# GpSimd's tap powers, VectorE's first statistics, the gated end and filler matmuls put in another order

## The reference

```python
def tblock(x, ...):                      # 4 heads of 8 channels, L0
    net = mha(x, qkv_w, proj_w, proj_b, rel_table, rel_idx) + x
    net = layernorm(net, ln_g, ln_b)
    return (net @ fc1_w.T + fc1_b) @ fc2_w.T + fc2_b + net

def L1(x, ...):
    h = einsum('bdl,de->ble', u, W_enc) + b_enc             # 32 -> 256
    dtA = A * dt[:, None]; Bd = (exp(dtA) - 1.0) / A
    vand = exp(dtA[:, :, None] * arange(16))
    K = 2.0 * einsum('dn,dnl->dl', Cc * Bd, vand).real      # 16 taps per channel
    y = gelu(causal_conv(h, K) + D * h)
    g = y @ W_glu + b_glu
    g = g[..., :256] * sigmoid(g[..., 256:])
    return layernorm(h + g, ln_gamma, ln_beta) @ W_dec + b_dec   # 256 -> 32

x = x + L0(group_norm(x))
x = x + L1(group_norm(x))
```

## Time and profile before

| | us |
|---|---|
| runs | 230.51, 227.83, 230.13 |
| median | 230.13 |
| the profiled execution | 230.15 |
| its span in the profile | 228.3 |
| PE, DVE, ACT, POOL busy | 196.2, 148.5, 128.2, 102.7 |
| filler matmuls (L1752), 84 of them, busy | 25.0 |
| mean granted TensorE clock | 0.924 |

### The profile page before, as it was taken

How to read it: one execution, slowest core, us unless ns; L and a number is a source line. 1 busy time by engine, 2 the same in 40 slices (tenths; PEclk the granted TensorE clock), 3 DMA queues, 4 the chain that set the end, 5 groups by cost and what they waited for, 6 DMA issues and landing times.

```text
span 228.3 us, 6295 instructions
## 1 busy us (share of the span) xinstructions
PE 196.2 (86%) x2533; PEld 103.2 (45%) x2533; DVE 148.5 (65%) x300; ACT 128.2 (56%) x248; POOL 102.7 (45%) x220
## 2 busy tenths in 40 slices
PE   0859989899896669898849877999999999999985
PEld 0334444445553224344335343445555566665582
DVE  0876566947654873649815698994233568898873
ACT  2273976775565663765503825873455765566550
POOL 6258443637860504707797230630000256776540
PEclk9985599999999985999958999999999999999985
DMA  5944500000000000200000000153000000000000
GB/s 169 190 122 106 122 3 4 4 3 3 3 0 3 0 3 3 90 6 3 4 0 4 0 0 3 34 132 78 0 0 0 0 3 1 14 10 10 10 13 20
DMA packets 3905, 6.70 MB, mean 29 GB/s; under 512 B 1605, under 2 KB 2869, under 8 KB 3781
## 3 DMA queue, kind: packets, MB, share of 16 engines
q1 hardware_dynamic: 2581, 3.91, 7.3%
q0 software_dynamic: 512, 1.37, 2.3%
q10 hardware_dynamic: 784, 1.03, 2.0%
HBM read 4.53 MB, written 0.40 MB: 22 GB/s over the span
## 4 chain that ended last, share of the span: by engine, by line
PE 59%; DVE 14%; issue 9%; POOL 8%; ACT 7%; DMA 2%; SPq 0%; DVEq 0%; POOLq 0%; ACTq 0%
PE ps L1864 13%; PE ps L1899 12%; PE ps L1752 3%; PE ps L1666 3%; DVE qs L1175 2%; PE ps L1644 2%; DVE ks L1175 2%; PE ps L1626 2%; PE ps L1687 2%; PE ps L1710 2%; PE ps L1656 2%; PE ps L1614 2%; DMA sel<-pick 2%; DVE x L1275 2%; PE ps L1935 2%
## 5 line engine op out<-in xcount | busy, mean ns | idle before, releaser
L1752 PE MATMUL ps<-fill 128*128 128x512 f16 x84 | 25.0, 416 | 5.9 <-DMA sel<-pick 5.9
L1216 DVE TENSOR_REDUCE mx<-ps 128x16 f32<-128x784 f32 (+3 forms) x18 | 15.9, 889 | 17.6 <-PE ps L1626 17.6
L882 ACT ACTIVATE pr<-ps 128x784 f32<-128x784 f32 (+3 forms) x18 | 13.7, 759 | 13.3 <-PE ps L1666 13.3
L764 POOL TENSOR_TENSOR pr<-pr 128x448 f16<-128x448 f32 x7 | 7.5, 1070 | 27.0 <-ACT pr L1061 27.0
L855 ACT CAST q_hi<-ps 128x392 f16<-128x392 f32 (+1 forms) x30 | 13.8, 511 | 10.1 <-PE ps L1580 9.6
L1037 ACT ACTIVATE pt<-ps,ybias 128x448 f32<-128x448 f32 x14 | 8.9, 634 | 13.0 <-PE ps L1864 12.0
L1899 PE MATMUL ps<-vm_buf,wglu_hi 128*128 128x448 f16 x56 | 15.1, 352 | 0.0
L1275 DVE STREAM_TRANSPOSE x<-u 96x448 f32<-96x448 f32 (+4 forms) x12 | 13.9, 1155 | 2.0 <-ACT u L935 1.7
L1752 PEld LDWEIGHTS ps<-fill 128*128 128x128 f16 x84 | 7.8, 107 | 14.3 <-issue 9.0
L1864 PE MATMUL ps<-u4hi,gw_hi 128*128 128x448 f16 x56 | 12.9, 353 | 1.6 <-ACT u4hi L1019 1.5
L895 ACT ACTIVATE den<-ps 128x196 f32<-128x196 f32 (+2 forms) x15 | 5.2, 346 | 15.6 <-PE ps L1692 15.6
(11 more groups left out here) (274 smaller groups left out, 544.0 us busy)
## 6 DMA issues: line engine op xcount, KB each, us to landing
xr<-x SPq DMA_DIRECT2D x3, 392.0 KB, 6.1
wglu<-w_glu POOLq DMA_DIRECT2D x1, 512.0 KB, 3.9
x<-x_win SPq DMA_DIRECT2D x4, 112.0 KB, 3.6
out<-u SPq DMA_DIRECT2D x7, 56.0 KB, 1.6
x<-x_win SPq DMA_DIRECT2D x2, 168.0 KB, 4.8
u4hi<-ust_s SPq DMA_DIRECT2D x4, 84.0 KB, 2.4
par_g<-stage_g POOLq DMA_DIRECT2D x1, 274.5 KB, 3.1
x<-x_win ACTq DMA_DIRECT2D x2, 112.0 KB, 6.3
```

Of the source, the lines that this page charges most:

```text
L882: nc.scalar.activation(dst[:, :, 0:cw], ps[:, 2:4, 0:cw], ACT.Exp).then_inc(s_exp[k], 1)
L1216: nc.vector.tensor_reduce(m[:, :, 0:n], ps[:, bank:bank + 2, 0:n * T].rearrange("p h (j m) -> p h j m", m=T), AX.X, ALU.max).then_inc(s_mx ...
L1752: nc.tensor.matmul(ps[:, 3, :], fill[:, 0:128], fill[:, :], start=True, stop=True)
```

## The change

It moves work and adds no arithmetic that the output needs. Its parts are:

1. GpSimd: level 1 of the tap powers runs ahead of `norm_halves("g", 0)`, and `wencst` is split behind `norm_halves("g", 1)`.
2. TensorE: the eight transposes of `gt` move from group 2 of block g to group 3, the last, ahead of its first `attend`.
3. TensorE: twelve more fillers at the front of each block: four between the bias matmuls and the products of the first scores, four ahead of the first turned scores, four ahead of the first bias matmuls of group 1.
4. VectorE, front: the tables from `sel` are split in two; the image's statistics come first, the sums of `sel` (`pick_sums`) behind them, `negsel` and `mask` (`pick_tables`) after `spread_projection("b")`. `repeat32` is made in `pick_sums`. TensorE's first fillers no longer wait for `sel`; there are 9 ahead of the statistics' matmul instead of 7, and 12 behind it, tied to two stages of the group norm, instead of 8.
5. The first half of block b's weights is issued as GpSimd's first instruction, not from ScalarE's queue.
6. Gated end, last chunk only: VectorE's `token_scale(n-2)` comes behind `gated_residual(n, 1)`, and TensorE's `decoded_back` of that chunk behind `mean_square_of_sum` of the last but one.

```diff
--- before.py
+++ after.py
...
+            pool.dma_start(par["b"][0:96, 0:288], stage_b[0:96, 0:288]).then_inc(s_pb, 16)
             nc.gpsimd.memset(eps[:, :], 1e-5).then_inc(s_eps, 1)
...
+            def enc_weights():
...
                 nc.gpsimd.tensor_copy(wencst[:, :], s4("wenc", 96)).then_inc(s_we, 1)
...
             first_tap()
...
-            tap_powers((0,))
+            tap_powers((0, 1))
             norm_halves("g", 0)
-            tap_powers((1, 2, 3))
+            tap_powers((2, 3))
             tap_weights()
             norm_halves("g", 1)
+            enc_weights()
             dec_weights()
...
-            act.dma_start(par["b"][0:96, 0:288], stage_b[0:96, 0:288]).then_inc(s_pb, 16)
...
             def group_norm_by_quarters():
...
-                nc.vector.tensor_tensor(repeat32[:, :], sel[:, 0:96], sel[:, 32:128], ALU.add)
...
+                pick_sums()
                 dve.wait_ge(s_gnm, 1)
...
-            def attention_constants():
+            def key_rows():
...
                 ins.then_inc(s_key, 1)
+                dve.wait_ge(s_key, 1)
+                for i in range(2):
+                    ins = nc.vector.tensor_copy(ones[:, i, :].rearrange("p (r w d) -> p r w d", r=2, w=2),
+                                                key_of[:, i, :].unsqueeze(1).unsqueeze(3).broadcast_to([128, 2, 2, 8]))
+                ins.then_inc(s_const, 1)
+            def pick_sums():
                 dve.wait_ge(s_sel, 16)
+                nc.vector.tensor_tensor(repeat32[:, :], sel[:, 0:96], sel[:, 32:128], ALU.add).then_inc(s_const, 1)
                 residue = sel[:, 0:64]
...
                 nc.vector.tensor_reduce(half_of[:, :], residue.rearrange("p (a l) -> p a l", a=2), AX.X,
...
-                dve.wait_ge(s_const, 1)
+            def pick_tables():
+                dve.wait_ge(s_const, 3)
                 nc.vector.tensor_scalar(negsel[:, :, :], head_of[:, :].unsqueeze(2).broadcast_to([128, HEADS, 64]),
...
                 nc.vector.scalar_tensor_tensor(out=mask[:, :].rearrange("p (j a) -> p j a", a=2),
...
-                                               op0=ALU.mult, op1=ALU.mult)
-                dve.wait_ge(s_key, 1)
-                for i in range(2):
-                    ins = nc.vector.tensor_copy(ones[:, i, :].rearrange("p (r w d) -> p r w d", r=2, w=2),
-                                              key_of[:, i, :].unsqueeze(1).unsqueeze(3).broadcast_to([128, 2, 2, 8]))
-                ins.then_inc(s_const, 1)
-                dve.wait_ge(s_const, 2)
+                                               op0=ALU.mult, op1=ALU.mult).then_inc(s_const, 1)
...
             def spread_max(k, g):
...
                 dve.wait_ge(s_mx[k], 2 * g + 2)
+                dve.wait_ge(s_const, 4)
...
-            attention_constants()
+            key_rows()
             group_norm_by_quarters()
...
                     spread_projection("b")
+                    pick_tables()
...
                 gated_residual(n, 0)
-                if n >= 2:
+                if 2 <= n < last:
                     token_scale(n - 2)
                 gated_residual(n, 1)
+                if n == last:
+                    token_scale(n - 2)
                 residual_lo(n)
                 if n >= 2:
...
                 nw = wide(k, g)
+                if u == 2:
+                    keep_running(4, bank)
...
                                      bt[k][:, h, 0:1, 0:T].broadcast_to([128, nw, T]), start=True, stop=True)
+                if u == 0:
+                    keep_running(4)
...
-                pe.wait_ge(s_const, 2)
+                pe.wait_ge(s_const, 4)
                 pe.wait_ge(s_mxe[k], g + 1)
...
-            def keep_running(count):
+            def keep_running(count, bank=3):
...
-                    nc.tensor.matmul(ps[:, 3, :], fill[:, 0:128], fill[:, :], start=True, stop=True)
+                    nc.tensor.matmul(ps[:, bank, :], fill[:, 0:128], fill[:, :], start=True, stop=True)
...
             def tap_weights():
...
             pe.wait_ge(s_fill, 1)
-            pe.wait_ge(s_sel, 16)
-            keep_running(7)
+            keep_running(9)
+            pe.wait_ge(s_const, 2)
             pe.wait_ge(s_gn, 3)
             nc.tensor.matmul(ps[0:96, 2, 0:2], repeat32[:, :], mean_q[:, :], start=True, stop=True).then_inc(s_gnm, 1)
-            keep_running(8)
+            keep_running(4)
+            pe.wait_ge(s_gnr, 3)
+            keep_running(5)
+            pe.wait_ge(s_uhi["b"], 1)
+            keep_running(3)
...
                 for g in range(groups[k]):
+                    if g == 0:
+                        keep_running(4)
                     turned_scores(k, g, 0)
...
                         scores(k, g + 1, 1)
-                    if k == "b" and g == last:
-                        fold_constant("g")
+                    if g == last:
+                        if k == "b":
+                            fold_constant("g")
+                        else:
+                            pe.wait_ge(s_mx[k], 2 * groups[k])
+                            tap_weights()
                     attend(k, g, 0)
...
-                    if g == last - 1:
+                    if k == "b" and g == last - 1:
                         pe.wait_ge(s_mx[k], 2 * groups[k])
-                        if k == "b":
-                            fold("g")
-                        else:
-                            tap_weights()
+                        fold("g")
...
-                if n >= 2:
+                if 2 <= n < last:
                     decoded_back(n - 2)
             decode(last - 1)
             mean_square_of_sum(last - 1)
+            decoded_back(last - 2)
             decode(last)
...
```

## The result

| | before | changed |
|---|---|---|
| runs, us | 230.51, 227.83, 230.13, 231.29 | 220.49, 219.06, 220.61, 219.88 |
| median | 230.32 | 220.19 |
| the profiled execution | 230.15 | 220.49 |
| its span | 228.3 | 218.7 |
| mean granted clock of it | 0.924 | 0.966 |

The changed kernel is faster: the ratio is 0.958, with a 95% interval of 0.953 to 0.963. The forecast was 220.2 us.

The account below looks back on a forecast made before the run. TensorE was taken to bound the kernel, busy 86% of the span, losing time in waits and 27.3 us at half clock. Gains of 5.5 + 2.2 + 2.0 + 0.3 = 10.0 us from 230.15 gave 220.2 us, range 217.0 to 225.5.

Parts of the forecast that it names:

- C: Front of block b: products start 0.65 us earlier and the slow stretch goes or shrinks; −2.0 us, bounds −6.5 and +1.2.
- B: Front of block g: twelve fillers keep the clock at 2.4 GHz; −2.2 us, bounds −3.4 and +2.7.
- A: Taps, block g: level 1 fills GpSimd's pause, so gt, yn and the feed-forward come earlier; −5.5 us.
- D: Gated end, last chunk: zt no longer delays the second gated_residual; −0.3 us, the middle of −0.6 and +0.15.
- The margin of 2.26 us: GpSimd's pause in block g: level 1 would end 2.26 us ahead of the rows it might delay.
- The 0.6 us that the working gave to the variance: In B: two f32 matmuls, some 0.6 us on a later group's path, absent at block g's front; raises 1.6 to 2.2.
- the bound for the low clock: In B: at half clock each filler takes 0.45 us, 1.8 for four, of which 0.9 would stick out.
- the cap: In C: earlier q and k gain no more than GpSimd's bias tables, ready at 14.25, allow; products start about 15.6.
- Only the taps gain: Both block fronts stay slow and the fillers are paid for: 228.3 us, or 226 with cheaper fillers; chance 0.12.
- The tap stall only moves: GpSimd's pause shrinks below 3.41 us and level 1 holds up norm_halves("g", 0): 228 us if lows stay; chance 0.04.
- The clock falls elsewhere: Half-clock stretches move or return in part; with one or two left over, 222 to 225.5 us; chance 0.26.
- Slower: Block b's fillers prolong half clock past 29.57, at 0.32 us lost per us; needs 45 us of it; chance 0.03.

Follow-up runs that it names:

- p_taps: The kernel before with the tap parts alone (level 1 earlier, wencst split, transposes in the last group): 224.77 us, ratio 0.983.
- p_lvl2: The changed kernel with level 2 of the tap powers also ahead of norm_halves("g", 0): 226.57 us, ratio 0.983.
- p_pool: The kernel before with GpSimd's new order alone, transposes left in group 2: 225.20 us, ratio 0.977.
- p_back: The changed kernel with the transposes put back between the attend halves of group 2: 219.95 us, ratio 0.955.
- p_fill: The kernel before with the 24 fillers in the two block fronts alone: 227.35 us, ratio 0.993.
- p_nofront: The changed kernel with the old front (VectorE's order, early fillers, weights' DMA on ScalarE's queue): 220.14 us, ratio 0.960.
- p_lvl2_fill: p_lvl2 with ten more fillers in the wait at the feed-forward of group 1 in block g: 222.49 us, ratio 0.966.
- p_more: p_back with ten more fillers in idle places ahead of the two block fronts: 219.59 us, ratio 0.956.
- p_end: p_back with three fillers in the gated end, ahead of the decoded_back that waits for zt: 220.67 us, ratio 0.959.
- p_tail: The kernel before with the gated end alone changed: one execution, 228.71 us.
- p_front: The kernel before with VectorE's front order, the early fillers and the weights' DMA on GpSimd's queue alone: 228.89 us, ratio 0.998.
- p_nofill: The changed kernel without the 24 fillers in the two block fronts: 222.99 us, ratio 0.970.

## Why the prediction was right, and where its steps were not

**The sum.** Forecast 10.0 us, measured 230.15 − 220.49 = 9.7 between the profiled executions and 10.1 between the medians. Its terms, read from the table of instants:

| term | forecast | measured |
|---|---|---|
| C, front of block b | −2.0 | −2.41 |
| B, front of block g | −2.2 | −1.43 |
| A, taps | −5.5 | −5.70 + 0.22 = −5.48 |
| D, gated end | −0.3 | −0.63 + 0.3 = −0.3 |

**A held in all its steps but one.** `gt`, the `yn` pair and the feed-forward fell where the working put them, and p_taps alone gave 5.3 us by the medians. The transposes took 1.09 us in the last group and cost 0.22. The margin of 2.26 us for GpSimd is right for the taps alone (2.44 us of pause are left in p_taps) and was too wide for the whole change: with the fronts faster its first `yn` pair came 3.84 us earlier (103.07, now 99.23), GpSimd's own work ahead of level 1 only 2.7, and 1.33 us were left. p_lvl2 shows what lay beyond it. The step that wasn't needed is the move of the transposes (p_pool, p_back): I had not asked whether the old place would do once `gt` was early.

**B had the right mechanism, the right price and one stretch too many.** With the clock at full all through, the front of block g takes 13.76 or 13.77 us in each of six traces (p_fill, p_nofront, p_back, p_lvl2_fill, p_more, p_end), against 16.02 before: 2.25 us. The 0.6 us that the working gave to the variance stood in no row; from the scores to the inverse of the sums p_fill has 87.64 − 83.74 = 3.90 us where before has 6.15, so the size was right. In the profiled execution of the changed kernel a slow stretch stood at 73.94 to 77.35, and four of the new fillers fell into it, at 74.78: 1.91 us, as the bound for the low clock has it. That cost the 0.8 us by which B came out short.

The rest of the forecast was that fillers in waits of 1 us keep the clock up. Of the fourteen traces, the six without the new fillers have 3.4 to 10.2 us of low clock at this front; of the eight with them, six have none and two (the changed kernel and p_lvl2) have 3.4 us. The length of the low stretch differs with the same work ahead: before, p_taps, p_pool and p_tail are the same kernel up to this front and have 6.8, 6.8, 10.2 and 3.4 us. The Trainium skill (TensorE: Matmul & The Clock Gate, Part 1) lays a fall of the clock to idle time. The third stretch of before, which went with its wait of 3.99 us in p_taps, agrees with it; the front of block g, where filling waits of about 1 us lifted the clock, is not explained by long idle time: its waits before were 1.36, 1.17 and 0.93 us.

**C came out near, by a wrong start.** The forecast had 0.65 us from the start and 1.35 from the clock. The clock's part was right: from block b's first products to the inverse of its first sums it is 29.20 − 16.24 = 12.96 us before and 26.79 − 15.13 = 11.66 in the changed kernel, 1.30 less, and 11.66 in p_fill and p_nofront too. The start gave 1.11, not 0.65. The step that failed is the cap, by which the first products hang on GpSimd's bias tables and the order of VectorE's statistics is worth nothing more. The row of before had them wait for VectorE's `ks`, and they follow it in the traces, whether the tables are early or not:

| | tables ready | `ks` ready | first products |
|---|---|---|---|
| before | 14.25 | 16.19 | 16.24 |
| changed | 12.94 | 15.07 | 15.13 |
| p_front | 13.31 | 15.23 | 15.29 |
| p_nofront | 14.30 | 15.95 | 16.00 |

In the changed kernel and p_nofront four of the fillers fill most of that wait. So the start came through q and k: before, TensorE's matmuls for them waited 2.04 us for VectorE's `ust_b`, until 13.01, and in the changed kernel they start at 11.68. That it is the statistics' place that did this, and not the other parts of the front, is argued, since no run has it alone. What would have shown C, products that wait for `bt`, did not come. The tables hold TensorE's bias matmuls up in p_back and p_more alone, by 0.26 and 0.55 us.

The tables themselves were to stay at 14.25, and did not. GpSimd's first rows in p_front:

```profile
11.49 0.66 POOL L548 CAST bt_b<-bias 49x196 f16<-49x196 f32 x2 [1.08 <-DMA bias<-tab_b]
...
12.24 1.07 POOL L552 TENSOR_TENSOR bt_b<-bias,bt_b 49x196 f16<-49x196 f32 x2
```

They were ready at 12.89 to 13.64 in the eight traces with the new front, and at 13.82 to 14.78 in the six with the old one, so this comes with the front and not by chance. The issues on SP's queue are the same. Whether it is the DMA that left ScalarE's queue, or VectorE's other order, is open, since no run parts the two.

**What the front is worth in the end is open as well.** p_nofront is as fast as the changed kernel. Its clock over six executions was 0.973 to 0.992, that of the changed kernel 0.966 to 0.984 over four, and that of p_back, with the same front, 0.972 to 0.980 over four. The six traces with the new front and the 24 fillers each have one or two low stretches of 3.4 us ahead of the gated end, beside the one behind p_lvl2's wait; of the two with the old front, p_nofront has none, and p_fill none at the fronts. So the 0.85 us won at the start may be given back by slow stretches that fall more often with this front; but two executions of p_end, with the new front, had a clock of 0.992, and the runs don't settle it.

**D** has the right total, but not for the reason given. The second `gated_residual` came 0.63 us earlier, and 0.3 of that was gone by the end of the span. The forecast took a middle because `residual_lo` might be delayed. It isn't: it starts 1.32 us behind the start of the second `gated_residual`'s last row in both kernels (219.39 − 218.07, 209.45 − 208.13). The traces point to the clock. From the start of the last chunk's first `gated_residual` to the end of the span it takes, in us:

| sums of squares of the last chunk | old order | new order |
|---|---|---|
| at full clock, 0.93 us | 12.7 (p_taps, p_pool) | 12.0 to 12.1 (p_tail, p_back, p_nofront, p_end) |
| at the low clock, 1.63 us | 13.2 (before) | 12.9 to 13.1 (changed, p_nofill, p_lvl2_fill, p_more) |

Where the low clock sets in behind these sums in both, the new order keeps all of its 0.6 us. These are differences between single traces; p_front (13.0), p_fill (13.6) and p_lvl2 (12.3) had it set in elsewhere.

`zt` took 0.39 us in its new place. The Trainium skill (GPSIMD Engine Reference, § 8. Key points) has the two engines contend for SBUF. By the forecast's reading of it `zt` would have stayed at 1.0; this did not happen, for only 0.25 us of it lay beside GpSimd's operation (207.95 to 208.98). The slow row of before (1.01) ran beside GpSimd's operations from start to end, so that the rule isn't contradicted.

**The rivals.** *Only the taps gain* falls with p_fill and p_nofill. *The tap stall only moves* did not happen, and p_lvl2 shows that it was mispriced: it was put at 228 us with the lows staying, and only the wait itself was reckoned with. At 2.4 us of lateness it cost 6.4 us. *The clock falls elsewhere* happened in a small way in the changed kernel, two stretches of 3.41 us, and in p_fill, where 6.8 us came up at 132. *Slower* did not; its price of 0.32 us for each us at the low clock, taken from block g, was too high for block b (1.30 / 13.65 = 0.10) and too low for the stretch in p_lvl2 (4.1 / 10.24 = 0.40).

## What to carry to other kernels

Where an engine pauses just ahead of its critical work, put later work into the pause in the pieces that the code has, and add up how much pause is left, with the shift of the engines in front of it counted: one piece too many cost here 6.4 us for a wait of 2.41. Price a wait of TensorE twice, by its own length and by the clock behind it, and put fillers into waits of 1 to 2.5 us when the work behind them is TensorE's; p_more and p_end show that more of them need not buy more. Before you cap a gain by another chain, read which one the wait in the row names: here it was `ks`, not the tables. After such a move, try the old place of what was moved along with it, since half of a change may not be needed.

## What the runs showed of the hardware

A wait of TensorE of 2.41 us was followed by 10.2 us at 1.2 GHz (p_lvl2), and the same wait with ten 128x512 matmuls on zeros in it by none (p_lvl2_fill); in time, 4.1 us. What a microsecond at the low clock costs depends on the place: those 10.2 us cost 4.1, the 6.83 at the front of block g 2.25, and the 13.65 at the front of block b 1.30 (p_fill against before), where VectorE and ScalarE have 8.31 and 8.72 us of work. Eight f32 transposes of 128x128 took 1.90 to 1.94 us at the low clock and 1.06 to 1.09 at the full one. Stretches at the low clock fall at other places and have other lengths from one kernel to the next, although the work there is the same: block b had one at 27.5 to 31 us in p_back and none in p_nofront, and block g's front had 3.4 us in p_tail and 10.2 in p_pool.
